# Moving two PSUM-to-SBUF copies of the softmax normalization from ScalarE to VectorE in an attention and FFN kernel

## The chip, the cores and the metric

The kernel runs on 8 NeuronCores of one Trainium2 chip. Each core takes one sequence of the batch of 8, with no exchange between cores. The metric is the device time in microseconds of the slowest core. A core has TensorE (matmuls; PE in the profile), ScalarE (ACT), VectorE (DVE), GpSimd (POOL) and SyncE (SP), which run their own instruction streams and wait for each other by semaphores; here GpSimd and SyncE only issue DMAs.

## What is computed

One transformer layer on x of shape (8, 4096, 1024), with 16 heads of 64. The reference, cut to what matters:

```python
q = _split_heads(x @ Wq + bq, h)
k = _split_heads(x @ Wk + bk, h)
v = _split_heads(x @ Wv + bv, h)
pattern = jnp.einsum('bhid,bhjd->bhij', k, q) * scale
prob = jax.nn.softmax(pattern, axis=-2)
out = jnp.einsum('bhis,bhid->bhsd', prob, v)
attn = concat @ Wo + bo
x = _layernorm(x + attn)
h = jax.nn.gelu(jnp.einsum('bse,eh->bsh', x, w1) + b1, approximate=False)
x = _layernorm(x + jnp.einsum('bsh,he->bse', h, w2) + b2)
```

## The kernel before

The kernel is written engine by engine: `tr.op("pe", ...)` appends an instruction to one engine's list and `tr.wait("pe", sem, value)` a wait in front of what comes next in that list. The order in which the Python code calls them is therefore the order of each engine's queue. On ScalarE and VectorE every instruction also waits for the one before it on the same engine (`AUTO_CHAIN`).

**First part (0 to about 750 us).** x is transposed, q, k and v are computed and written to scratch in HBM, and the weights are cast to bf16. The change does not touch it.

**Second part.** The 4096 queries are cut in 8 chunks (`qc`) of 512, and the 16 heads are taken in 8 pairs (`p`). So there are 64 head-pair blocks. In a block the keys come in 32 chunks (`kc`) of 128. For each of them TensorE computes the scores of both heads (`scores`, L799) into one of two PSUM tiles `ps_s`; ScalarE takes the exponential of a 128x1024 tile (`do_exp`, L812) into one of two SBUF tiles `es_sb`; TensorE then adds into `ps_o` the product with v (`pv`, L822) and into `ps_d` the product with ones, which is the softmax's denominator (`denom`, L834). In the loop over `kc` the order on TensorE is pv(kc), denom(kc), scores(kc+2).

`ps_o` and `ps_d` are single PSUM tiles. At the end of a block (L860 to L877) they are copied to SBUF (`dD_sb` at L864, `oO_sb` at L865), VectorE takes the reciprocal of `dD_sb` (L867) and multiplies it with `oO_sb` for the two heads (L869, L872) into `o_sb`. The value `norm_done` stands for the second copy; `pv(0)` of the next block waits for it (L819), since it writes `ps_o` again. Ahead of `pv(0)` stand, on TensorE, scores(0) and scores(1) of the next block. On ScalarE exp(0) of the next block stands behind the two copies.

**The work pumped in between.** While the blocks of chunk `qc` run, a generator (`make_post`) emits the rest of the layer for chunk `qc-1`: output projection (L635), layer norm (`emit_ln_tail`, L553 to L609), first FFN matmul (L668, eviction on VectorE at L679), Gelu on ScalarE in two batches of 128x8192 (L686), second FFN matmul (L712, L724), second layer norm (L606) and four output transposes (L741) with their copies (L747) and the DMA of the single buffer `out_sb`. `pump(n)` takes n pieces from it: one after every odd `kc` (kc = 31 too), two more at kc = 3, and one at the very end of a block, after the normalization. That makes 19 pieces per block; the generator has 107, so the pieces end within the block p = 5, and chunk `qc` = 0 has none. At the boundary behind block p (its last pumped piece before the normalization and the one after it) stand: for p = 0 two pieces of the first layer norm's last loop, for p = 1 two chunks of the first FFN matmul, for p = 2 the last such chunk with the second Gelu and a piece of the second matmul, for p = 3 two pieces of the second matmul, for p = 4 an empty piece and the start of the second layer norm's last loop, for p = 5 and 6 nothing. Behind p = 7 the 8 loads of the next chunk's `q_sb` are issued on GpSimd when the last block's matmuls are done.

Of the kernel before, what the change touches and what calls it, by code (L numbers as in the profile page):

```python
# [75 lines left out]
def build(debug=(), phases="AB", nqc=NQC, nst=NST, sparts="LTAV"):  # L76
# [36 lines left out]
    with ExitStack() as st0:  # L113
        tr = Tracer(nc, st0)
        SB = lambda *a: st0.enter_context(nc.sbuf_tensor(*a))
        PS = lambda *a: st0.enter_context(nc.psum_tensor(*a))
        pe, act, dve = "PE", "ACT", "DVE"
# [356 lines left out]
        dD_sb = SB("dD_sb", [128, 512], F32)  # L474
        oO_sb = SB("oO_sb", [128, 512], F32)

        ps_s = [PS("ps_s0", [128, 1024], F32), PS("ps_s1", [128, 1024], F32)]
        ps_o = PS("ps_o", [128, 512], F32)
        ps_d = PS("ps_d", [128, 512], F32)
# [29 lines left out]
        norm_done = 0  # L509
        o_last = 0  # L510
# [6 lines left out]
        def load_kv(p):  # L517
            b = p % 2
            tr.wait("gp", pe, free_k[b])
            v_k[b] = tr.op("gp", lambda e, p=p, b=b: e.dma_start(  # L520
                k_sb[b][:], bass.AP(k_d.tensor, p * 128 * S, [[S, 128], [1, S]])),
                sem=f"s_k{b}", n=16)
            tr.wait("gp", pe, free_v[b])
            v_v[b] = tr.op("gp", lambda e, p=p, b=b: e.dma_start(
                v_sb[b][:], bass.AP(v_d.tensor, p * 128 * S, [[S, 128], [1, S]])),
                sem=f"s_v{b}", n=16)
# [230 lines left out]
        def pump(n=1):  # L757
            nonlocal post_gen
            for _ in range(n):
                if post_gen is None:  # L760
                    return
                try:
                    next(post_gen)
                except StopIteration:
                    post_gen = None
                    return

        def load_q(qc):
            nonlocal v_q
            tr.wait("gp", pe, free_q)  # L770
            for pc in range(NP):
                v_q = tr.op("gp", lambda e, pc=pc, qc=qc: e.dma_start(
                    q_sb[:, pc * 512:(pc + 1) * 512],
                    bass.AP(q_d.tensor, pc * 128 * S + qc * 512, [[S, 128], [1, 512]])),
                    sem="s_qb", n=16)

        for qc in qc_range:
            post_gen = make_post(qc - 1) if qc > 0 else None
            if qc == 0:
                tr.wait("pe", dve, v_ones64)  # L780
                load_q(0)
                load_kv(0)
                load_kv(1)
            for p in range(NP):
                b = p % 2
                if 1 <= p < NP - 1:
                    load_kv(p + 1)
                elif p == NP - 1 and qc + 1 in qc_range:
                    load_kv(0)
                sc_done = {}  # L790
                exp_done = {}

                def scores(kc, p=p, b=b):
                    if kc == 0:
                        tr.wait("pe", f"s_k{b}", v_k[b])
                        tr.wait("pe", "s_qb", v_q)
                    v = None
                    for hh in range(2):
                        fn = lambda e, p=p, b=b, kc=kc, hh=hh: e.matmul(  # L799
                            ps_s[kc % 2][:, hh * 512:(hh + 1) * 512],  # L800
                            k_sb[b][hh * 64:(hh + 1) * 64, kc * 128:(kc + 1) * 128],
                            q_sb[hh * 64:(hh + 1) * 64, p * 512:(p + 1) * 512],
                            start=True, stop=True, tile_position=(hh * 64, 0))
                        v = tr.op("pe", fn, sem=(pe if hh == 1 else None))
                    sc_done[kc] = v

                def do_exp(kc):
                    esb = kc % 2
                    tr.wait("act", pe, es_free.get(esb, 0))
                    tr.wait("act", pe, sc_done[kc])  # L810
                    exp_done[kc] = tr.op(
                        "act", lambda e, kc=kc, esb=esb: e.activation(  # L812
                            es_sb[esb][:], ps_s[kc % 2][:], AF.Exp, scale=SCALE))

                def pv(kc, p=p, b=b):
                    tr.wait("pe", act, exp_done[kc])
                    if kc == 0:
                        tr.wait("pe", f"s_v{b}", v_v[b])
                        tr.wait("pe", act, norm_done)  # L819
                    esb = kc % 2  # L820
                    for hh in range(2):
                        tr.op("pe", lambda e, b=b, kc=kc, esb=esb, hh=hh: e.matmul(  # L822
                            ps_o[hh * 64:(hh + 1) * 64, :],
                            v_sb[b][:, kc * 128 + hh * 64: kc * 128 + (hh + 1) * 64],
                            es_sb[esb][:, hh * 512:(hh + 1) * 512],
                            start=(kc == 0), stop=(kc == NKC - 1),
                            skip_group_check=True,
                            tile_position=(0, hh * 64)))

                def denom(kc):  # L830
                    esb = kc % 2
                    v = None
                    for hh in range(2):
                        fn = lambda e, kc=kc, esb=esb, hh=hh: e.matmul(  # L834
                            ps_d[hh * 64:(hh + 1) * 64, :],
                            ones64[:],
                            es_sb[esb][:, hh * 512:(hh + 1) * 512],
                            start=(kc == 0), stop=(kc == NKC - 1),
                            skip_group_check=True,
                            tile_position=(0, hh * 64))  # L840
                        v = tr.op("pe", fn, sem=(pe if hh == 1 else None))
                    return v

                scores(0)
                do_exp(0)
                scores(1)
                vmm = 0
                for kc in range(NKC):
                    pv(kc)
                    vmm = denom(kc)  # L850
                    es_free[kc % 2] = vmm
                    if kc + 2 < NKC:
                        scores(kc + 2)
                    if kc + 1 < NKC:
                        do_exp(kc + 1)
                    if kc % 2 == 1:
                        pump(1)
                    if kc == 3:
                        pump(2)
                free_k[b] = vmm  # L860
                free_v[b] = vmm
                tr.wait("act", pe, vmm)
                tr.wait("act", dve, o_last)
                tr.op("act", lambda e: e.copy(dD_sb[:], ps_d[:]))  # L864
                norm_done = tr.op("act", lambda e: e.copy(oO_sb[:], ps_o[:]))  # L865
                tr.wait("dve", act, norm_done)
                tr.op("dve", lambda e: e.reciprocal(r_sb[:], dD_sb[:]))  # L867
                pcol = p * 512
                tr.op("dve", lambda e, pcol=pcol, qc=qc: e.tensor_tensor(  # L869
                    o_sb[qc % 2][0:64, pcol:pcol + 512],  # L870
                    oO_sb[0:64, :], r_sb[0:64, :], ALU.mult))
                o_last = tr.op("dve", lambda e, pcol=pcol, qc=qc: e.tensor_tensor(  # L872
                    o_sb[qc % 2][64:128, pcol:pcol + 512],
                    oO_sb[64:128, :], r_sb[64:128, :], ALU.mult))
                if p == NP - 1:
                    free_q = vmm
                pump(1)  # L877
            o_ready[qc] = o_last
            if qc + 1 in qc_range:
                load_kv(1)  # L880
                load_q(qc + 1)
            while post_gen is not None:
                pump(4)
# [56 lines left out]
```

How the kernel before makes its waits and increments, by code:

```python
    def wait(self, stream, sem, value):  # L49
        if value <= 0 or sem not in self.semh:
            return
        h = self.semh[sem]
        self.streams[stream].append(lambda e, h=h, v=value: e.wait_ge(h, v))
# [3 lines left out]
    def op(self, stream, fn, sem=None, n=1):  # L57
        ch = self.AUTO_CHAIN.get(stream)
        if ch is not None:
            self.wait(stream, ch, self.semv[ch])
            if sem is None:
                sem, n = ch, 1
            assert sem == ch
        if sem is None:
            self.streams[stream].append(fn)
            return None
        if sem not in self.semh:
            self._mk(sem)
        self.semv[sem] += n
        h = self.semh[sem]
        self.streams[stream].append(
            lambda e, fn=fn, h=h, n=n: fn(e).then_inc(h, n))
        return self.semv[sem]
```

## Time and profile before

| what | value |
|---|---|
| two timed runs | 4686.57 and 4742.26 us, median 4714.41 |
| the profiled execution | 4687.85 us |
| its span on the slowest core (core 4) | 4686.1 us |
| spans of the 8 cores | 4664.0 to 4686.1 us |
| TensorE busy | 3631.7 us (78%), 19264 matmuls |
| ScalarE busy | 2382.2 us (51%), 2319 instructions |
| VectorE busy | 1403.3 us (30%), 1814 instructions |
| mean granted TensorE clock, core 4 | 0.899 of 2.4 GHz |

The span runs from the first to the last instruction of a core; the time of an execution holds it and about 2 us around it. Matmul ends are modelled, so two matmuls in a row may overlap in the rows. A row's "idle before" is the time that its engine did nothing ahead of it, and behind "<-" stands what ended that idle time. A granted clock of 1.00 is 2.4 GHz, and where the engine is throttled it runs at 1.2 GHz; a value between is a mean over a stretch with both.

### The profile page before, as it was taken

The numbers are of one execution on the slowest core, as the hardware profiler recorded it, in microseconds if no ns is written. First come the engines' busy times: TensorE is split into PE (matmuls) and PEld (weight loads), VectorE is DVE, ScalarE is ACT, GpSimd is POOL, SyncE is SP. The second block draws the span as 40 slices with busy tenths as digits, with TensorE's granted clock in tenths as the row PEclk, the third lists the DMA queues.
The fourth block names the chain that finished last, engine by engine and source line by source line (L and its number), as shares of the span: only waits on it lengthen the run. The fifth ranks groups of instructions, "written<-read, shape, count | busy, mean of one in ns | idle before, by whom it ended". The sixth has DMA issues, their size and how long they took to land.

```text
span 4686.1 us, 57913 instructions; the slowest of 8 cores (4664.0 to 4686.1 us)
## 1 busy us (share of the span) xinstructions
PE 3631.7 (78%) x19264; PEld 1205.7 (26%) x19264; DVE 1403.3 (30%) x1814; ACT 2382.2 (51%) x2319; POOL 194.3 (4%) x344
## 2 busy tenths in 40 slices
PE   5365697777897799778887888788878887888766
PEld 2132242222232233222222222222222222222222
DVE  1132341114222422332233323332323232423243
ACT  0000005885557555755576556665666556655610
POOL 0010100000000000000000000000000000000000
PEclk9677798998999899989998999899999998989987
DMA  8766422113432243123412342234222322332143
GB/s 175 177 156 161 122 65 93 55 55 90 108 77 77 84 102 90 71 89 82 110 59 84 91 110 68 84 86 104 79 84 79 90 82 90 89 84 84 50 91 76
DMA packets 746248, 433.77 MB, mean 93 GB/s; under 512 B 679269, under 2 KB 695781, under 8 KB 728553
## 3 DMA queue, kind: packets, MB, share of 16 engines
q1 hardware_dynamic: 706714, 237.12, 20.6%
q0 software_dynamic: 39248, 192.96, 13.9%
q8 instruction: 164, 2.69, 0.3%
q14 instruction: 122, 1.00, 0.1%
HBM read 377.59 MB, written 77.59 MB: 97 GB/s over the span
## 4 chain that ended last, share of the span: by engine, by line
PE 61%; ACT 16%; DMA 9%; DVE 6%; issue 6%; POOL 1%; ACTq 0%; SPq 0%; DVEq 0%; POOLq 0%
ACT es_sb L812 12%; PE ps_o L822 12%; PE ps_s L799 10%; PE ps_d L834 7%; PE ps_w L712 5%; PE ps_w L668 5%; PE ps_g L712 5%; PE ps_g L668 5%; PE psq L318 3%; PE psq L422 2%; ACT h_sb L686 2%; PE psv L345 2%; DMA xt_f<-xtf_b 2%; DMA wcast<-w 2%; DMA y<-out_sb 1%
## 5 line engine op out<-in xcount | busy, mean ns | idle before, releaser
L812 ACT ACTIVATE es_sb<-ps_s 128x1024 bf16<-128x1024 f32 x2048 | 2097.4, 1024 | 1381.5 <-PE ps_s L799 1232.5
L822 PE MATMUL ps_o<-es_sb,v_sb 128*64 128x512 bf16 x4096 | 874.3, 417 | 399.9 <-ACT es_sb L812 399.4
L799 PE MATMUL ps_s<-q_sb,k_sb 64*128 64x512 bf16 x4096 | 832.3, 409 | 106.1 <-DMA q_sb<-q_scr 86.1
L834 PE MATMUL ps_d<-es_sb,ones 128*64 128x512 bf16 x4096 | 853.6, 400 | 0.0
L822 PEld LDWEIGHTS ps_o<-es_sb,v_sb 128*64 128x64 bf16 x4096 | 257.5, 108 | 1057.0 <-issue 1054.1
L867 DVE RECIPROCAL r_sb<-dD_sb 128x512 f32<-128x512 f32 x64 | 214.6, 3353 | 1037.8 <-ACT oO_sb L865 1037.1
L799 PEld LDWEIGHTS ps_s<-q_sb,k_sb 64*128 64x128 bf16 x4096 | 193.6, 94 | 997.9 <-issue 997.9
L712 PE MATMUL ps_w<-h_sb,w_sb 128*128 128x512 bf16 x1024 | 260.9, 406 | 77.2 <-ACT h_sb L686 77.2
L668 PE MATMUL ps_w<-h1b_sb,w_sb 128*128 128x512 bf16 x1024 | 259.5, 399 | 44.3 <-DVE h1b_sb L602 36.9
L278 ACT COPY xtf_b<-pst 128x512 f32<-128x512 f32 x64 | 37.5, 587 | 478.2 <-PE pst L270 277.6
L834 PEld LDWEIGHTS ps_d<-es_sb,ones 128*64 128x64 bf16 x4096 | 260.5, 112 | 2.9
L668 PE MATMUL ps_g<-h1b_sb,w_sb 128*128 128x512 bf16 x1024 | 243.7, 381 | 1.2 <-DMA w_sb<-w_scr 1.0
L712 PE MATMUL ps_g<-h_sb,w_sb 128*128 128x512 bf16 x1024 | 238.6, 380 | 0.0
L679 DVE TENSOR_SCALAR hpre_sb<-ps_w,b_pp 128x512 bf16<-128x512 f32 x128 | 96.1, 751 | 388.6 <-PE ps_w L668 316.4
L270 PE MATMUL pst<-id_f,xnat 128*128 128x128 f32 x256 | 53.4, 370 | 202.5 <-ACT xtf_b L278 173.0
L679 DVE TENSOR_SCALAR hpre_sb<-ps_g,b_pp 128x512 bf16<-128x512 f32 x128 | 96.1, 751 | 294.4 <-PE ps_g L668 286.4
L520 POOL DMA_DIRECT2D k_sb<-k_scr x64 | 34.0, 532 | 3269.3 <-PE ps_d L834 1854.8
L318 PE MATMUL psq<-xt_bf,wq_sb 128*128 128x512 bf16 x512 | 128.9, 419 | 33.6 <-DVE xpart L289 33.6
L712 PEld LDWEIGHTS ps_w<-h_sb,w_sb 128*128 128x128 bf16 x1024 | 96.9, 102 | 216.3 <-issue 129.8
L668 PEld LDWEIGHTS ps_w<-h1b_sb,w_sb 128*128 128x128 bf16 x1024 | 94.5, 101 | 179.4 <-issue 93.2
L686 ACT ACTIVATE h_sb<-hpre_sb 128x8192 bf16<-128x8192 bf16 x16 | 112.5, 7029 | 30.0 <-DVE hpre_sb L679 29.8
L668 PEld LDWEIGHTS ps_g<-h1b_sb,w_sb 128*128 128x128 bf16 x1024 | 92.2, 98 | 124.5 <-issue 29.6
(94 smaller groups left out, 2225.4 us busy)
## 6 DMA issues: line engine op xcount, KB each, us to landing
k_sb<-k_scr POOLq DMA_DIRECT2D x64, 1024.0 KB, 5.2
v_sb<-v_scr POOLq DMA_DIRECT2D x64, 1024.0 KB, 7.5
w_sb<-w_scr SPq DMA_DIRECT2D x256, 256.0 KB, 3.0
w_sb<-w_scr SPq DMA_DIRECT2D x128, 512.0 KB, 4.4
xnat<-x SPq DMA_DIRECT2D x8, 2048.0 KB, 12.3
xt_f<-xtf_b SPq DMA_DIRECT2D x64, 256.0 KB, 2.2
w_scr<-wcast SPq DMA_DIRECT2D x64, 256.0 KB, 3.7
wo_sb<-wo_scr SPq DMA_DIRECT2D x64, 256.0 KB, 3.8
```

What stands on the lines that cost most here:

```text
L318: fn = lambda e, fc=fc, cc=cc, stp=stp, qb=qb: e.matmul(psq[qb][:], wq_sb[:, cc * E + fc * 128: cc * E + (fc + 1) * 128], xt_bf[cc][:, stp ...
L345: tr.op("pe", lambda e, j=j, cc=cc, stp=stp, vb=vb, half=half: e.matmul(psv[vb][:, half * 512:(half + 1) * 512], xt_bf[cc][:, stp * 512 + ...
L422: fn = lambda e, fc=fc, cc=cc, stp=stp, qb=qb: e.matmul(psq[qb][:], wk_sb[:, cc * E + fc * 128: cc * E + (fc + 1) * 128], xt_bf[cc][:, stp ...
L668: fn = lambda e, cc=cc, wb=wb, pb=pb: e.matmul(pwb[pb][:], w1_sb[wb][:, cc * 128:(cc + 1) * 128], h1b_sb[:, cc * 512:(cc + 1) * 512], star ...
L679: last_pw[pb] = tr.op("dve", lambda e, hc=hc, pb=pb: e.tensor_scalar(hpre_sb[:, (hc % 16) * 512:(hc % 16 + 1) * 512], pwb[pb][:], b1_pp[:, ...
L686: "act", lambda e, hc=hc: e.activation(h2_sb[:, (hc - 15) * 512:(hc + 1) * 512], hpre_sb[:], AF.Gelu))
L712: fn = lambda e, hc=hc, wb=wb, pb=pb: e.matmul(pwb[pb][:], w2_sb[wb][:, (hc % 16) * 128:(hc % 16 + 1) * 128], h2_sb[:, hc * 512:(hc + 1) * ...
L799: fn = lambda e, p=p, b=b, kc=kc, hh=hh: e.matmul(ps_s[kc % 2][:, hh * 512:(hh + 1) * 512], k_sb[b][hh * 64:(hh + 1) * 64, kc * 128:(kc + ...
L812: "act", lambda e, kc=kc, esb=esb: e.activation(es_sb[esb][:], ps_s[kc % 2][:], AF.Exp, scale=SCALE))
L822: tr.op("pe", lambda e, b=b, kc=kc, esb=esb, hh=hh: e.matmul(ps_o[hh * 64:(hh + 1) * 64, :], v_sb[b][:, kc * 128 + hh * 64: kc * 128 + (hh ...
L834: fn = lambda e, kc=kc, esb=esb, hh=hh: e.matmul(ps_d[hh * 64:(hh + 1) * 64, :], ones64[:], es_sb[esb][:, hh * 512:(hh + 1) * 512], start= ...
L867: tr.op("dve", lambda e: e.reciprocal(r_sb[:], dD_sb[:]))
```

## The change

The two copies at the end of a block move from ScalarE's list to VectorE's, directly ahead of the reciprocal. With them the waits change: VectorE waits for the last `denom` itself, no longer for ScalarE's copy, ScalarE waits for nothing at this place, and `pv(0)` waits for VectorE's counter instead of ScalarE's.

```diff
@@ -816,7 +816,7 @@
                     tr.wait("pe", act, exp_done[kc])
                     if kc == 0:
                         tr.wait("pe", f"s_v{b}", v_v[b])
-                        tr.wait("pe", act, norm_done)
+                        tr.wait("pe", dve, norm_done)
@@ -859,11 +859,9 @@
                 free_k[b] = vmm
                 free_v[b] = vmm
-                tr.wait("act", pe, vmm)
-                tr.wait("act", dve, o_last)
-                tr.op("act", lambda e: e.copy(dD_sb[:], ps_d[:]))
-                norm_done = tr.op("act", lambda e: e.copy(oO_sb[:], ps_o[:]))
-                tr.wait("dve", act, norm_done)
+                tr.wait("dve", pe, vmm)
+                tr.op("dve", lambda e: e.tensor_copy(dD_sb[:], ps_d[:]))
+                norm_done = tr.op("dve", lambda e: e.tensor_copy(oO_sb[:], ps_o[:]))
                 tr.op("dve", lambda e: e.reciprocal(r_sb[:], dD_sb[:]))
```

On ScalarE, from the end of the first part on, the blocks of chunk 0 stand like this before (`es_sb` is the exponential, one block is x32):

```order
L278 COPY xtf_b<-pst 128x512 x64
L812 ACTIVATE es_sb<-ps_s 128x1024 x32
L864 COPY dD_sb<-ps_d 128x512
L865 COPY oO_sb<-ps_o 128x512
L812 ACTIVATE es_sb<-ps_s 128x1024 x32
L864 COPY dD_sb<-ps_d 128x512
L865 COPY oO_sb<-ps_o 128x512
```

and after the change, up to the first Gelu of chunk 1:

```order
L278 COPY xtf_b<-pst 128x512 x64
L812 ACTIVATE es_sb<-ps_s 128x1024 x275
L575 ACTIVATE stB<-stA 1x512
L577 ACTIVATE stA<-stB 1x512
L812 ACTIVATE es_sb<-ps_s 128x1024 x50
L686 ACTIVATE h_sb<-hpre_sb 128x8192
```

The exponentials of one block now follow directly on those of the block before. Line numbers ahead of L862 are the same in both kernels; behind it they are 2 lower after the change (the copies are L863 and L864, the reciprocal L865).

On VectorE the boundary behind block p = 1 of chunk 1 stands like this before, between evictions of the first FFN matmul (`hpre_sb`):

```order
L679 TENSOR_SCALAR hpre_sb<-ps_w,b_pp 128x512
L867 RECIPROCAL r_sb<-dD_sb 128x512
L869 TENSOR_TENSOR o_sb<-oO_sb,r_sb 64x512
L872 TENSOR_TENSOR o_sb<-oO_sb,r_sb 64x512
L679 TENSOR_SCALAR hpre_sb<-ps_g,b_pp 128x512
```

and after the change:

```order
L679 TENSOR_SCALAR hpre_sb<-ps_w,b_pp 128x512
L863 COPY dD_sb<-ps_d 128x512
L864 COPY oO_sb<-ps_o 128x512
L865 RECIPROCAL r_sb<-dD_sb 128x512
L867 TENSOR_TENSOR o_sb<-oO_sb,r_sb 64x512
L870 TENSOR_TENSOR o_sb<-oO_sb,r_sb 64x512
L679 TENSOR_SCALAR hpre_sb<-ps_g,b_pp 128x512
```

The copies stand behind the eviction of the piece pumped at kc = 31 and ahead of that of the piece pumped after the normalization.

## Rows read from the trace of the kernel before

**Rows 1.** The page's chain that ended last, shares by engine.

```profile
PE 61%; ACT 16%; DMA 9%; DVE 6%; issue 6%; POOL 1%; ACTq 0%; SPq 0%; DVEq 0%; POOLq 0%
```

**Rows 2.** Groups of instructions by line: busy us, mean ns | idle before, releasers.

```profile
L864 ACT COPY dD_sb<-ps_d 128x512 f32<-128x512 f32 x64 | 37.5, 586 | 71.5 <-PE ps_d L834 60.1 <-DVE hpre_sb L679 9.6 <-PE ps_s L799 1.3
...
L357 DVE CAST v_b<-psv 128x1024 bf16<-128x1024 f32 x32 | 39.2, 1224 | 102.1 <-PE psv L350 95.7 <-DMA v_scr<-v_b 6.3
...
L591 DVE COPY mrb_sb<-ps_g 128x512 f32<-128x512 f32 x16 | 11.1, 692 | 1.6
```

**Rows 3.** Chain of waits, 949 to 953 us (bare boundary): start us, us, what.

```profile
949.42 0.59 ACT dD_sb L864
...
950.09 0.59 ACT oO_sb L865
...
950.77 1.03 ACT es_sb L812
```

**Rows 4.** Timeline of the same boundary, TensorE: start us, us, instruction, [idle before].

```profile
948.81 0.41 PE L834 MATMUL ps_d<-es_sb,ones 128*64 128x512 bf16 x2
...
949.15 0.61 PE L799 MATMUL ps_s<-q_sb,k_sb 64*128 64x512 bf16 x4
...
952.15 0.41 PE L822 MATMUL ps_o<-es_sb,v_sb 128*64 128x512 bf16 x2 [2.39 <-ACT es_sb L812]
```

**Rows 5.** The 21 stretches between bare boundaries: us, busy us, PEclk, DMA, GB/s.

```profile
788.12:828.86 40.74, 32.44 (x194) 8.52 (x196) 4.73 (x3) 33.94 (x34) 1.05 (x2) 0.92 0.14 52
...
949.22:988.22 39.00, 30.09 (x194) 8.44 (x196) 4.72 (x3) 33.94 (x34) 1.05 (x2) 1.00 0.14 55
...
sum 841.65, PE 665.82 PEld 178.11 DVE 99.25 ACT 712.77 POOL 22.14; mean PE 31.71 PEld 8.48 DVE 4.73 ACT 33.94 POOL 1.05
```

**Rows 6.** The 14 us behind boundary p = 1, first of 14.

```profile
1201.58:1215.60 14.02, 12.70 (x67) 4.71 (x68) 7.72 (x7) 6.57 (x8) 1.05 (x2) 1.00 0.76 229
```

**Rows 7.** Timeline of VectorE, then TensorE, boundary p = 1 of chunk 2.

```profile
1682.74 0.75 DVE L679 TENSOR_SCALAR hpre_sb<-ps_w,b_pp 128x512 bf16<-128x512 f32 x1 [2.07 <-PE ps_w L668]
1683.60 3.35 DVE L867 RECIPROCAL r_sb<-dD_sb 128x512 f32<-128x512 f32 x1
...
1688.64 0.75 DVE L679 TENSOR_SCALAR hpre_sb<-ps_g,b_pp 128x512 bf16<-128x512 f32 x1
...
1686.08 0.41 PE L822 MATMUL ps_o<-es_sb,v_sb 128*64 128x512 bf16 x2 [1.32 <-ACT es_sb L812]
...
1691.45 1.90 PE L668 MATMUL ps_g<-h1b_sb,w_sb 128*128 128x512 bf16 x8
```

**Rows 8.** Timeline of VectorE, then TensorE, after boundary p = 0 of chunk 2.

```profile
1624.61 3.35 DVE L867 RECIPROCAL r_sb<-dD_sb 128x512 f32<-128x512 f32 x1 [3.11 <-ACT oO_sb L865]
...
1637.60 0.43 DVE L602 CAST h1b_sb<-h1f_sb 128x512 bf16<-128x512 f32 x1
...
1638.39 1.89 PE L668 MATMUL ps_w<-h1b_sb,w_sb 128*128 128x512 bf16 x8 [2.65 <-DVE h1b_sb L602]
```

**Rows 9.** Timeline of VectorE, then TensorE, after boundary p = 4 of chunk 2.

```profile
1896.34 0.69 DVE L591 COPY mrb_sb<-ps_g 128x512 f32<-128x512 f32 x1
1898.16 3.35 DVE L867 RECIPROCAL r_sb<-dD_sb 128x512 f32<-128x512 f32 x1 [1.13 <-ACT oO_sb L865]
...
1915.13 0.69 DVE L606 TENSOR_TENSOR h1f_sb<-sq_sb,mrb_sb 128x512 f32<-128x512 f32 x1
...
1916.39 0.66 PE L741 MATMUL ps_w<-id_f,h1f_sb 128*128 128x128 f32 x4
...
1921.55 0.63 PE L741 MATMUL ps_w<-id_f,h1f_sb 128*128 128x128 f32 x4 [2.31 <-DMA y<-out_sb]
```

**Rows 10.** Timeline: ScalarE behind p = 2, TensorE behind p = 7.

```profile
1769.33 1.28 ACT L812 ACT_TABLE_LOAD   x1 [3.26 <-PE ps_s L799]
...
1081.10 1.04 PE L799 MATMUL ps_s<-q_sb,k_sb 64*128 64x512 bf16 x4 [14.24 <-DMA q_sb<-q_scr]
```

**Rows 11.** A stretch of the first FFN matmul after its wait for `h1b_sb`.

```profile
1157.70:1169.20 11.50, 11.44 (x56) 3.55 (x58) 2.17 (x3) 4.10 (x4) 0.00 (x0) 0.85 0.20 46
```

## The prediction

> **What bounds the kernel now.** I began with the page's chain of work that ended last: TensorE holds 61% of it and ScalarE 16%, VectorE 6% [rows 1]. That is an average over unlike stretches, so I looked at the one place where the moved copies stand, the boundary between two head pairs, after `denom(31)` of one pair and before `pv(0)` of the next. There are 64, and they are of several kinds. The chain of waits through a boundary in which nothing of the FFN is pumped reads copy of `ps_d`, copy of `ps_o`, exp(0), then `ps_o` matmul, without a hole [rows 3]: ScalarE works through two copies of 0.59 us before it may start the exp that TensorE needs. TensorE has its scores done in 0.61 us and then sits idle for 2.39 us [rows 4]. So at such a boundary ScalarE's queue sets the pace. Inside a pair ScalarE paces as well (one exp per about 1.1 us), so what is won at the boundary isn't taken back by the following exps.
>
> The second thing at this place is the clock of TensorE. The stretches from one such boundary to the next last 39.00 us where the granted clock is 1.00 (2.4 GHz all through) and 40.74 where it is 0.92, since the engine fell to 1.2 GHz for a part of it [rows 5]. The 2.39 us at the boundary are the only long idle in such a stretch. There are 21 such stretches (7 in the first query chunk, p = 5 and 6 in the seven others); 18 of them show a clock under 1.00, and their sum is 841.65 us [rows 5]. At 39.00 each they would take 819.0, so the low clock costs 22.7 us there.
>
> **The change, part by part.** *Two copies leave ScalarE.* 64 times 2 copies of 586 ns [rows 2], 75 us of ScalarE. *Two copies come to VectorE.* The trace has this form, PSUM to SBUF, 128x512 f32, at line 591: 692 ns [rows 2]. Two with the 0.10 us between VectorE's instructions (1682.74 + 0.75 = 1683.49, next at 1683.60 [rows 7]) are 1.48 us. VectorE no longer waits for ScalarE before the reciprocal. *The wait of `pv(0)`* is now for VectorE's second copy, and ScalarE's copies waited for nothing else that mattered.
>
> *Bare boundary, VectorE idle (21 of them).* Take the one at 949.22, where `denom(31)` ends (948.81 + 0.41 [rows 4]). ScalarE answered 0.20 us later, at 949.42 [rows 3]. VectorE starts then too if it answers as fast, ends the copies at 950.90, and TensorE can go 0.36 us later, as after the cast that ends at 1638.03 (matmul at 1638.39 [rows 8]): 951.26. exp(0) now starts after scores(0), whose pair ends at about 949.54, plus about 0.16: 949.70 to 950.72; plus the 0.35 from the end of exp to the matmul (951.80 [rows 3] to 952.15 [rows 4]) 951.07. The later one counts: 951.26 against 952.15 [rows 4], so 0.89 us are saved and the new last wait is VectorE's copy, by 0.19 us. 21 x 0.89 = 18.7 us. Bounds of the copy: were it as short as ScalarE's, exp(0) would decide and 1.08 us be saved; were it as long as VectorE's 128x1024 cast out of PSUM, 1224 ns [rows 2], `pv(0)` would start at 952.32, 0.17 later than now. I take 0.69, since the row has the same shape, type and memories.
>
> *Boundary p = 0 of chunks 1 to 7 (7).* TensorE also gains 0.89 us here, but it runs into the layer norm: at the first `ps_w` matmul of line 668 it sits idle 2.65 us for the last cast of `h1b_sb`, which ends at 1638.03 at the end of an unbroken row of VectorE work from the reciprocal at 1624.61 on [rows 8]. The reciprocal started 1.63 us after `denom(31)` (ScalarE's second copy ends at 950.68, 1.46 us after it [rows 3], and VectorE follows in 0.17); now it starts at 0.20 + 1.48 + 0.10 = 1.78. The gain is swallowed, and the row ends 0.15 us later: 7 x 0.15 = 1.1 us lost.
>
> *Boundary p = 4 (7).* VectorE is still at line 591 until 1897.03, so the copies run to 1898.61 and the reciprocal starts at 1898.71 instead of 1898.16, 0.55 later. The second layer norm ends at 1915.82 [rows 9]; now at 1916.37, and the first transpose of line 741, at 1916.39 before, comes at 1916.73. Behind it TensorE waits for the output DMA of the single `out_sb` (idle 2.31 us before the next transpose [rows 9]), so this delay is handed on and the gain at the boundary lost: 7 x 0.35 = 2.5 us lost.
>
> *Boundaries p = 1 and 3 (14).* 16 matmuls of the FFN stand between `denom(31)` and the scores, TensorE idles only 1.32 us and for exp(0) [rows 7]. At p = 1 VectorE first has an eviction that ends at 1683.49; the copies end at 1685.07, TensorE could start at 1685.43, before 1686.08. Nothing gained or lost. The eviction behind the normalization slips from 1688.64 to about 1690.2 and ends at 1690.97; the matmul that needs its bank starts at 1691.45 [rows 7]. That cover is thin, 0.48 less 0.36 us; if it goes, some tenths of a us are lost seven times.
>
> *Boundaries p = 2 (7) and p = 7 (7).* At p = 2 exp(0) waits for scores behind the Gelu and a table load, which starts at 1769.33, 3 us after the copies ended [rows 10]; at p = 7 TensorE idles 14.24 us for `q_sb` [rows 10]. Both hide the copies before and after. Nothing. The last boundary adds 0.15 us before the final output projection.
>
> Direct sum: 18.7 - 1.1 - 2.5 - 0.1 = 15.0 us.
>
> *The clock.* The idle at the bare boundary shrinks from 2.39 to 1.50 us. Where it is 1.32 us today (p = 1 and 3) the granted clock stays at 1.00 in the 14 us from the boundary on, in all 14 places (the first is shown [rows 6]), though TensorE is denser around those (busy 12.7 of 14 us). 1.50 is much nearer to the 1.32 that never drops it than to the 2.39 that did 18 times in 21. I take three quarters of the 22.7 us back: 17 us; the bounds are 0 and 22.7.
>
> The page TensorE: Matmul & The Clock Gate of the Trainium skill (section A second HAM failure mode: psum-queue depth-cycling) says that short, frequent idles of TensorE between groups of matmuls make its clock swing between the levels. By it a boundary with 1.5 us idle could still drop it, the second case below; the rows of p = 1 and 3 disagree with it, the 18 of 21 agree.
>
> Against the profiled execution: 4687.85 (span 4686.1) - 15.0 - 17 = 4656 us, 0.7% less. The two timed runs of before are 4686.57 and 4742.26, median 4714.41: the profiled one lies at the low end, and the same saving from the median would give 4682. Differences within 2% (94 us) are about what a measurement of this kernel can't tell from no change.
>
> **The rivals.** *B, the clock still falls.* The copies leave the path, but the idle of 1.50 us drops the clock as before. For it: 18 of 21 today, with loosely packed matmuls. Against it: rows 6. 4687.85 - 15.0 = 4673.
>
> *C, slower: the stretches of layer norm and FFN give it back.* Place: p = 0 and p = 4. TensorE reaches line 668 up to 0.89 us earlier plus what the clock gave, and waits 3.5 us or more instead of 2.65 for VectorE. What follows are dense matmuls, where a drop costs more; one such stretch after the wait had a clock of 0.85 over 11.5 us [rows 11], that is 3.4 us at 1.2 GHz and 1.7 us lost. One more such drop at each of 14 places costs 24 us; if at the same time nothing comes back at the bare boundaries, -15 + 24 = +9: 4697. It decides from 9 extra drops on (15 / 1.7). Against it: six of the seven FFN stretches already begin at 0.85, so most have paid. The long copy of 1224 ns would end at the same side: 21 x 0.17, and 1.2 us at each of 7 + 7, together +20: 4708.
>
> *D, all of it.* exp(0) decides, no drop is left, and VectorE's slip hides: 21 x 1.08 + 22.7 = 45.4: 4642. The change does what it says in any case: ScalarE's row of exps is unbroken in the new order.
>
> **How the numbers follow.** Forecast 0.52, B 0.20, D 0.13, C together with the long copy 0.12, anything else 0.03. Range 4636 to 4710: D less 6 us, since the cores of one execution lie 22 us apart, up to the long copy, which also covers B and C from an execution nearer to the median. Faster by over 2% would need 94 us, twice D: 0.03. Slower by over 2% would need 1.5 us at every one of the 64 boundaries: 0.02. Within 2%: 0.95.
>
> **What would show it.** At bare boundaries: `ps_o` idle near 1.5 us, released by VectorE's `oO_sb`; copies of 0.69 us starting 0.20 us after `denom(31)`; stretches of 38.1 us at clock 1.00. At p = 0: idle before line 668 up to 3.5 us, reciprocal 1.78 us after `denom(31)`. It is wrong if the copy takes over 0.8 us, if bare stretches stay above 39 us (the clock), if a new wait shows at line 668 behind p = 1, or if the sum of the 21 stretches falls by less than 15 us.

## The result, and the profile after the change

The changed kernel takes 4662.2 us (median of 27 runs) against 4692.21 us for the kernel before (26 runs). The ratio is 0.9923, with a 95% interval from 0.9903 to 0.9943: 0.8% less time, a small difference but clear of the noise. Executions in which the cores of one die ran longer at a lower clock than the other's are left out of every ratio in this document (not out of the medians), and where too few others were left no ratio is given. The profiled execution of the changed kernel took 4654.42 us.

From the page of the changed kernel, its head, the engines and the shares of the chain that ended last:

```profile
span 4652.6 us, 57786 instructions; the slowest of 8 cores (4623.5 to 4652.6 us)
...
PE 3600.3 (77%) x19264; PEld 1204.8 (26%) x19264; DVE 1491.7 (32%) x1942; ACT 2305.6 (50%) x2191; POOL 193.7 (4%) x344
...
PE 59%; ACT 14%; DVE 10%; DMA 9%; issue 6%; POOL 1%; ACTq 0%; DVEq 0%; SPq 0%; POOLq 0%
```

VectorE's share of the chain rose from 6% to 10% and ScalarE's fell from 16% to 14% [rows 1]. The groups by line (busy us, mean ns | idle before, releasers) price the moved work:

```profile
L863 DVE COPY dD_sb<-ps_d 128x512 f32<-128x512 f32 x64 | 44.3, 692 | 847.2 <-PE ps_d L834 845.1
L864 DVE COPY oO_sb<-ps_o 128x512 f32<-128x512 f32 x64 | 44.2, 691 | 6.6
```

A copy costs 692 ns on VectorE, 106 ns more than on ScalarE, exactly the row of line 591 [rows 2]. At a bare boundary the profile's chain of waits now names VectorE (start, us, what):

```profile
942.70 0.23 PE ps_d L834 x2
...
943.09 0.70 DVE dD_sb L863
943.89 0.70 DVE oO_sb L864
944.59 0.19 issue
944.77 0.41 PE ps_o L822 x2
```

And the timeline of the same place, all three engines:

```profile
942.85 0.60 PE L799 MATMUL ps_s<-q_sb,k_sb 64*128 64x512 bf16 x4
943.09 0.69 DVE L863 COPY dD_sb<-ps_d 128x512 f32<-128x512 f32 x1 [31.11 <-PE ps_d L834]
943.40 2.14 ACT L812 ACTIVATE es_sb<-ps_s 128x1024 bf16<-128x1024 f32 x2 [1.25 <-PE ps_s L799]
943.89 0.69 DVE L864 COPY oO_sb<-ps_o 128x512 f32<-128x512 f32 x1
944.77 0.41 PE L822 MATMUL ps_o<-es_sb,v_sb 128*64 128x512 bf16 x2 [1.32 <-DVE oO_sb L864]
```

TensorE's idle is 1.32 us instead of 2.39 [rows 4]. The profile puts its end down to VectorE's second copy, since that is what ended last (944.58). But the last wait is still exp(0), by 0.05 us. In front of `pv(0)` stand three waits in TensorE's list: for exp(0), for `v_sb` and, behind them, for the copy. From the end of exp(0) to the matmul it is 0.356 us before the change, where the copies had long ended, and 0.356 us after it (medians over the 8 cores): the copy adds nothing. When the copy does decide, as in e2 below, the matmul follows it by 0.146 us; here it follows by 0.198.

The windows of the 21 bare stretches (us, busy of each engine, PEclk, DMA share, GB/s), first one and sum:

```profile
792.34:829.98 37.64, 30.09 (x195) 8.43 (x196) 6.11 (x5) 32.75 (x32) 1.05 (x2) 1.00 0.15 57
...
sum 790.60, PE 631.71 PEld 176.17 DVE 128.26 ACT 687.72 POOL 22.03; mean PE 30.08 PEld 8.39 DVE 6.11 ACT 32.75 POOL 1.05
```

All 21 of this core are at a clock of 1.00 (on the eight cores together 160 of 168; before the change 41 of 168), and their sum fell from 841.65 [rows 5] to 790.60 us. Something was given back at p = 0, at the first `ps_w` matmul of line 668 (to be read against [rows 8]):

```profile
1612.23 3.35 DVE L865 RECIPROCAL r_sb<-dD_sb 128x512 f32<-128x512 f32 x1
...
1625.22 0.43 DVE L602 CAST h1b_sb<-h1f_sb 128x512 bf16<-128x512 f32 x1
...
1626.01 3.57 PE L668 MATMUL ps_w<-h1b_sb,w_sb 128*128 128x512 bf16 x8 [4.50 <-DVE h1b_sb L602]
```

The wait is 4.50 us where it was 2.65, and the eight matmuls behind it take 3.57 us where they took 1.89.

To compare whole kernels I cut each core's timeline at the end of the last `denom` of every head pair, and take the mean over the eight cores, in us. "At 1.2 GHz" is the time in which the clock records show the lower level.

| | before | after |
|---|---|---|
| span | 4673.5 | 4635.9 |
| 21 bare stretches | 836.9 | 791.4 |
| of them at 1.2 GHz | 76.8 | 3.4 |
| stretches p = 0 (7) | 408.1 | 416.7 |
| p = 1 (7) | 513.4 | 512.1 |
| p = 2, 3 (7 each) | 999.0 | 999.6 |
| p = 4 (7) | 352.4 | 355.1 |
| p = 7 (6), and p = 7 of chunk 0 | 518.2 | 516.8 |
| up to the first boundary, and from the last | 1045.2 | 1044.0 |

A stretch "p" begins at the end of head pair p. Behind p = 1, 2 and 4 the cut stands some 0.4 us too early in every kernel, at the end of `denom(30)` (1680.23 in the kernel before, where `denom(31)` ends at 1680.66). So the rows p = 0 come out 3 us too short and those of p = 4 some 3 us too long, in all kernels alike; cut at `denom(31)`, p = 0 takes 411.2 and 419.8 us and p = 4 349.0 and 352.0. The differences between kernels hold. The bare stretches gain 45.5 us, p = 0 and p = 4 lose 8.6 and 2.7, the rest moves by a few: 37.6 in all.

### The profile page after: what moved, and what is told of

It is laid out like the page before. It is cut to its first block, busy times and chain, and to the rows that moved or that the text cites. A ratio compares the mean times of both kernels' runs of the same rounds, so it can differ in the third digit from the quotient of the medians.

```text
span 4652.6 us, 57786 instructions; the slowest of 8 cores (4623.5 to 4652.6 us)
## 1 busy us (share of the span) xinstructions
PE 3600.3 (77%) x19264; PEld 1204.8 (26%) x19264; DVE 1491.7 (32%) x1942; ACT 2305.6 (50%) x2191; POOL 193.7 (4%) x344
## 4 chain that ended last, share of the span: by engine, by line
PE 59%; ACT 14%; DVE 10%; DMA 9%; issue 6%; POOL 1%; ACTq 0%; DVEq 0%; SPq 0%; POOLq 0%
ACT es_sb L812 11%; PE ps_o L822 11%; PE ps_s L799 9%; PE ps_d L834 7%; PE ps_w L668 5%; PE ps_w L712 5%; PE ps_g L712 5%; PE ps_g L668 5%; PE psq L318 3%; PE psq L422 2%; ACT h_sb L686 2%; PE psv L345 2%; DMA xt_f<-xtf_b 2%; DMA wcast<-w 2%; DVE r_sb L865 2%
## 5 line engine op out<-in xcount | busy, mean ns | idle before, releaser
L822 PE MATMUL ps_o<-es_sb,v_sb 128*64 128x512 bf16 x4096 | 858.6, 409 | 373.0 <-ACT es_sb L812 313.7
L799 PE MATMUL ps_s<-q_sb,k_sb 64*128 64x512 bf16 x4096 | 818.5, 402 | 106.4 <-DMA q_sb<-q_scr 85.4
L834 PE MATMUL ps_d<-es_sb,ones 128*64 128x512 bf16 x4096 | 837.7, 392 | 0.0
L863 DVE COPY dD_sb<-ps_d 128x512 f32<-128x512 f32 x64 | 44.3, 692 | 847.2 <-PE ps_d L834 845.1
L865 DVE RECIPROCAL r_sb<-dD_sb 128x512 f32<-128x512 f32 x64 | 214.5, 3352 | 6.9 <-DVE oO_sb L864 0.5
L724 DVE SCALAR_TENSOR_TENSOR y_sb<-ps_w,b_pp,h1f_sb 128x512 f32<-128x512 f32 x32 | 24.0, 751 | 325.6 <-PE ps_w L712 324.9
```

Source lines behind the costliest of these rows:

```text
L799: fn = lambda e, p=p, b=b, kc=kc, hh=hh: e.matmul(ps_s[kc % 2][:, hh * 512:(hh + 1) * 512], k_sb[b][hh * 64:(hh + 1) * 64, kc * 128:(kc + ...
L822: tr.op("pe", lambda e, b=b, kc=kc, esb=esb, hh=hh: e.matmul(ps_o[hh * 64:(hh + 1) * 64, :], v_sb[b][:, kc * 128 + hh * 64: kc * 128 + (hh ...
L834: fn = lambda e, kc=kc, esb=esb, hh=hh: e.matmul(ps_d[hh * 64:(hh + 1) * 64, :], ones64[:], es_sb[esb][:, hh * 512:(hh + 1) * 512], start= ...
```

## The experiments

My theory: the gain has two terms, about 1 us of latency at each bare boundary and a clock that no longer falls there; and it is limited by VectorE's row of work at p = 0 and p = 4. The rivals: the clock is only a passenger of the order; the thin covers at p = 1 and p = 4 (little time between VectorE's work and the matmul that needs it) matter more; the loss at p = 0 is VectorE's 0.13 us and not the clock.

**e1: the kernel before, with TensorE's idle filled.** The extra matmuls' results are used nowhere.

```diff
             scores(1)
+            if (qc == 0 and p >= 1) or (qc > 0 and p >= 6):
+                tr.wait("pe", dve, last_pw[1])
+                for _ in range(6):
+                    tr.op("pe", lambda e, p=p, b=b: e.matmul(
+                        ps_g[:], k_sb[b][:, 0:128],
+                        q_sb[:, p * 512:(p + 1) * 512],
+                        start=True, stop=True))
```

> The kernel before, with six extra matmuls (bf16, 128x512, into ps_g, which nothing reads then) on TensorE between scores(1) and pv(0) at the 21 bare boundaries. They fill 1.3 us of the 2.39 us idle and shorten no wait; pv(0) still starts 2.93 us after denom(31). Theory (the clock is a term of its own): with 1.1 us idle the clock stays at 1.00 in the 21 stretches, their sum falls from 836.9 (mean of the cores before) to about 819 or less, and the time falls by some 18 us (ratio about 0.996). Rival (the gain of the change comes only from the shorter wait): the stretches keep their 837 us and the ratio is 1.000, or above it by the extra work.

Measured: ratio 0.9948 [0.9933, 0.9963]. ScalarE's copies stand where they stood, and still the bare stretches fall from 836.9 to 816.6 us (mean of the cores). Windows of one core:

```profile
909.82:948.55 38.73, 31.50 (x201) 8.94 (x202) 4.73 (x3) 33.94 (x34) 1.05 (x2) 1.00 0.14 55
948.55:987.56 39.01, 31.49 (x201) 8.93 (x202) 4.73 (x3) 33.94 (x34) 1.05 (x2) 1.00 0.14 54
...
sum 816.84, PE 661.46 PEld 187.09 DVE 99.24 ACT 712.79 POOL 22.05; mean PE 31.50 PEld 8.91 DVE 4.73 ACT 33.94 POOL 1.05
```

No stretch is below 1.00. On none of the eight cores is there any time at 1.2 GHz in them. The clock is a term of its own, of 20.3 us; the remaining 25.2 us down to the 791.4 of the change are what the moved copies bring beside the clock. (The mean span of the profiled execution is only 10.9 us shorter, 4662.6 us: its first part, which has the same code, happened to take 5.7 us more.) Two lengths, 38.73 and 39.01 us, stand at the same clock; the last section takes that up.

**e2: VectorE's copies back on the path.** The change, with the first copy made twice.

```diff
                 tr.op("dve", lambda e: e.tensor_copy(dD_sb[:], ps_d[:]))
+                tr.op("dve", lambda e: e.tensor_copy(dD_sb[:], ps_d[:]))
                 norm_done = tr.op("dve", lambda e: e.tensor_copy(oO_sb[:], ps_o[:]))
```

> The changed kernel, with the copy of ps_d made twice on VectorE ahead of the copy of ps_o. pv(0) at the bare boundaries moves from 1.86 to 2.65 us after denom(31), the idle from 1.32 to 2.11. Theory: 0.79 us lost directly at each of 21 boundaries (16.6 us), and the clock falls again at more than half of them (0.6 to 1.7 us each, some 10 to 20 us); with 0.8 us at the layer norm boundaries the ratio to before is about 1.000 to 1.003. Rival (clock untouched by the idle below the old 2.39): 16.6 + 5.5 us lost, ratio 0.997, granted clock 1.00 in all 21 stretches.

Measured: ratio 1.0042 [1.0022, 1.0061], slower than before. Windows of one core:

```profile
788.34:826.73 38.39, 30.03 (x194) 8.39 (x196) 6.80 (x6) 32.80 (x32) 1.05 (x2) 1.00 0.16 55
826.73:865.99 39.26, 31.30 (x195) 8.47 (x196) 6.80 (x6) 32.80 (x32) 1.05 (x2) 0.96 0.15 54
...
1023.25:1063.52 40.27, 32.54 (x193) 8.48 (x192) 6.80 (x6) 32.80 (x32) 1.05 (x2) 0.92 0.14 53
...
sum 824.89, PE 656.65 PEld 177.11 DVE 142.81 ACT 688.72 POOL 22.04; mean PE 31.27 PEld 8.43 DVE 6.80 ACT 32.80 POOL 1.05
```

The waits at one boundary of the same core:

```profile
945.15 2.14 ACT L812 ACTIVATE es_sb<-ps_s 128x1024 bf16<-128x1024 f32 x2 [1.25 <-PE ps_s L799]
...
946.43 0.69 DVE L865 COPY oO_sb<-ps_o 128x512 f32<-128x512 f32 x1
...
947.27 0.64 PE L822 MATMUL ps_o<-es_sb,v_sb 128*64 128x512 bf16 x2 [2.06 <-DVE oO_sb L865]
```

The stretch at full clock grows from 37.64 to 38.39 us, by 0.75, though VectorE's copies end 0.79 us later (0.69 and the 0.10 between instructions). The missing 0.05 is the margin by which exp(0), and not the copy, had been the last wait in the change; now it is the copy. TensorE's idle is 2.06 us, 0.05 less than the 2.11 expected; the low level is back (16 of the 21 stretches of this core are below 1.00; 77.5 us of it as the mean of the cores, as before), and nothing is left of the clock term. Against the change, VectorE's longer row also costs 12.5 us at p = 4, 5.7 at p = 1 and 3.3 at p = 0.

**e3b: VectorE's row longer, the path not.** One more instruction of 0.69 us behind the second copy; the reciprocal overwrites its result. (A first form, e3, wrote to a tile of its own, for which SBUF has no room: 2048 B are needed and 1824 left. It gave no time.)

```diff
                 norm_done = tr.op("dve", lambda e: e.tensor_copy(oO_sb[:], ps_o[:]))
+                tr.op("dve", lambda e: e.tensor_tensor(
+                    r_sb[:], dD_sb[:], dD_sb[:], ALU.mult))
                 tr.op("dve", lambda e: e.reciprocal(r_sb[:], dD_sb[:]))
```

> The changed kernel, with one more VectorE instruction of 0.69 us (dD_sb times itself into r_sb, overwritten by the reciprocal) behind norm_done and ahead of the reciprocal. pv(0) at the bare boundaries stays at 1.86 us. Theory (VectorE's row decides at p = 0 and 4): the first matmul of line 668 at p = 0 and the transposes at p = 4 come 0.79 us later, and p = 1 loses its thin cover; 12 to 20 us lost against the changed kernel, ratio to before 0.995 to 0.997, the 21 bare stretches unchanged at 791 us. Rival (the loss there comes from the clock alone): 0.992.

Measured: ratio 0.998 [0.9958, 1.0002]. The bare stretches take 795.0 us, 3.6 more than in the change; against the change p = 4 loses 14.1 us, p = 1 8.7 and p = 0 4.2, while the others gain some 8, for which I have no reason. In the waits of the slowest core (us in all, times, longest) that for the cast at p = 0 has grown and a new one, the second line, stands at p = 1, seven times:

```profile
PE ps_w L668 <- DVE h1b_sb L602: 58.8, 8, 19.0
...
PE ps_g L668 <- DVE hpre_sb L679: 3.1, 7, 0.8
```

3.1 us of waiting don't make 8.7; the time at 1.2 GHz in the stretches p = 1 rises too, from 47.8 to 65.7 us.

The ratio lies a little above the 0.995 to 0.997 expected. In mean spans 0.79 us more on VectorE between two pairs takes back 23.2 of the 37.6 us (4659.1 against 4635.9), nearly all of it away from the bare boundaries. There the path is the same, with an idle of 1.32 us, and still 37 of the 168 bare stretches show a lowered clock, 25 of them behind p = 5; in the change it was 8. So VectorE's row is a limit of its own, and I had priced the covers at p = 1 and p = 4 too low.

**e4: the reciprocal moved off VectorE's row.** The change, with the normalization of pairs 0 to 6 issued 21 key chunks later, inside the next pair.

```diff
+                    if kc == 21 and pending is not None:
+                        pending()
+                        pending = None
...
+                def normalize(pcol=p * 512, qc=qc):
+                    nonlocal o_last
...
+                if p == NP - 1:
+                    normalize()
+                else:
+                    pending = normalize
```

> The changed kernel, with the reciprocal and the two products of blocks p = 0 to 6 moved behind kc = 21 of the next block; only the two copies stay at the boundary (p = 7 as it was). Theory (the wait of 4.5 us at line 668 behind p = 0 is VectorE's reciprocal and products standing ahead of the layer norm's last four pieces): the row ends 4.7 us earlier, TensorE does not wait there, the clock stays up, 4.5 + 1.7 us saved in 7 chunks; at p = 4 the second layer norm ends 4.7 us earlier and up to 1.5 us per chunk are saved. Together 40 to 50 us, ratio to before about 0.983. Rival (something else holds line 668, or the deferred work delays the evictions it now stands among): ratio 0.99 to 1.00, with waits of TensorE for hpre_sb evictions in the profile.

Measured: ratio 0.9811 [0.9788, 0.9835], 4608.99 us: the fastest of all kernels here. Timeline and windows of p = 0 on one core:

```profile
1606.36 0.43 DVE L602 CAST h1b_sb<-h1f_sb 128x512 bf16<-128x512 f32 x1
...
1607.61 1.90 PE L668 MATMUL ps_w<-h1b_sb,w_sb 128*128 128x512 bf16 x8
```

```profile
1596.63:1649.46 52.83, 49.81 (x287) 16.11 (x288) 21.92 (x29) 32.74 (x32) 1.06 (x2) 1.00 0.35 95
...
sum 368.21, PE 348.89 PEld 112.99 DVE 153.50 ACT 229.17 POOL 7.42; mean PE 49.84 PEld 16.14 DVE 21.93 ACT 32.74 POOL 1.06
```

The cast ends 0.82 us before the matmul that reads it, no wait stands at line 668, and the clock is 1.00. p = 0 takes 368.6 us where the change alone takes 416.7 (means of the cores). The bare stretches take 2.9 us more than in the change: 31 of 168 show a lowered clock, 26 of them behind p = 5, again with an idle of 1.32 us. So the wait at line 668 was the place where the change's gain stopped.

**e5: one copy on each engine**, `ps_d` by ScalarE and `ps_o` by VectorE. `pv(0)` waits for both, which puts a fourth wait in front of it (not in the lines shown).

```diff
+                tr.wait("act", pe, vmm)
+                tr.wait("act", dve, o_last)
+                norm_a = tr.op("act", lambda e: e.copy(dD_sb[:], ps_d[:]))
                 tr.wait("dve", pe, vmm)
-                tr.op("dve", lambda e: e.tensor_copy(dD_sb[:], ps_d[:]))
                 norm_done = tr.op("dve", lambda e: e.tensor_copy(oO_sb[:], ps_o[:]))
+                tr.wait("dve", act, norm_a)
```

> The changed kernel, with the copy of ps_d back on ScalarE and the copy of ps_o on VectorE, side by side. exp(0) starts 0.88 us after denom(31) and pv(0) at 2.25 (idle 1.71 us instead of 1.32); the reciprocal starts at 0.97 instead of 1.76. Theory: 21 x 0.39 = 8 us lost directly at the bare boundaries and some more by the clock (an idle of 1.71 lies between the 1.32 that never drops it and the 2.11 that does), 5 to 12 us won at p = 0, 1 and 4 by VectorE's shorter row; ratio to before 0.990 to 0.997, granted clock under 1.00 in some of the 21 stretches, not in all. Rival (idle does not decide the clock): all 21 at 1.00.

Measured: no ratio; the profiled execution took 4666.02 us. Windows of one core:

```profile
792.54:830.65 38.11, 30.06 (x195) 8.40 (x196) 5.42 (x4) 33.36 (x33) 1.05 (x2) 1.00 0.14 56
...
947.15:986.17 39.02, 31.36 (x195) 8.47 (x196) 5.42 (x4) 33.37 (x33) 1.05 (x2) 0.96 0.15 55
...
sum 816.05, PE 650.25 PEld 176.90 DVE 113.74 ACT 700.70 POOL 22.03; mean PE 30.96 PEld 8.42 DVE 5.42 ACT 33.37 POOL 1.05
```

At a boundary of the same core:

```profile
948.03 2.14 ACT L813 ACTIVATE es_sb<-ps_s 128x1024 bf16<-128x1024 f32 x2
...
949.52 0.41 PE L824 MATMUL ps_o<-es_sb,v_sb 128*64 128x512 bf16 x2 [1.83 <-ACT es_sb L813]
```

exp(0), the first of the two (it ends at 949.06), is now behind one copy. TensorE idles 1.83 us, not the 1.71 expected: 0.46 us pass between the end of exp(0) and the matmul instead of 0.36, since the added wait stands behind that for exp(0). 13 of the 21 stretches show a lowered clock (8 stand at 1.00); on the eight cores it is 97 of 168. That is a point between the change and before, and it tells why the change is worth more than its microsecond. p = 0 takes 401.2 us, less than with either kernel.

**e7: the wait at p = 0 filled.** The change, with 16 matmuls (results unused) in front of line 668 for the layer norm that follows p = 0.

```diff
+            if pq < 7:
+                tr.wait("pe", dve, max(last_pw))
+                for _ in range(16):
+                    tr.op("pe", lambda e: e.matmul(
+                        pwb[0][:], wo_sb[0][:, 0:128], osrc[:, 0:512],
+                        start=True, stop=True))
```

> The changed kernel, with 16 extra matmuls (128x512, into ps_w, overwritten) on TensorE inside its wait of 4.5 us for h1b_sb at p = 0 of chunks 1 to 7. They end before the wait does. Theory (most of what is given back at p = 0 is the clock that this longer wait drops ahead of dense matmuls): the clock stays at 1.00 behind the wait, 6.8 us at 1.2 GHz less per chunk, that is 3.4 us x 7 = 24 us less, ratio to before about 0.987. Rival (the give-back is the later end of VectorE's row only, 0.13 us per chunk): ratio 0.992 as the changed kernel.

Measured: ratio 0.9886 [0.9857, 0.9914]; p = 0 401.9 us, 14.8 less than with the change. The cut at line 668 shows it best. Windows from its first matmul behind p = 0 to the next boundary, the second of seven and the sum, for one core each of the kernel before, of the change, and of e7:

```profile
1638.39:1680.23 41.84, 41.84 (x234) 13.96 (x236) 8.56 (x12) 22.53 (x22) 0.00 (x0) 1.00 0.31 70
...
sum 302.34, PE 302.33 PEld 99.05 DVE 60.00 ACT 157.71 POOL 0.00; mean PE 43.19 PEld 14.15 DVE 8.57 ACT 22.53 POOL 0.00
```

```profile
1626.01:1669.93 43.92, 43.92 (x234) 14.33 (x236) 8.56 (x12) 22.51 (x22) 0.00 (x0) 0.95 0.29 67
...
sum 308.10, PE 308.09 PEld 100.30 DVE 59.98 ACT 157.58 POOL 0.00; mean PE 44.01 PEld 14.33 DVE 8.57 ACT 22.51 POOL 0.00
```

```profile
1616.32:1658.16 41.84, 41.20 (x230) 13.95 (x236) 8.56 (x12) 22.53 (x22) 0.00 (x0) 1.00 0.31 70
...
sum 292.90, PE 288.45 PEld 97.69 DVE 60.00 ACT 157.73 POOL 0.00; mean PE 41.21 PEld 13.96 DVE 8.57 ACT 22.53 POOL 0.00
```

The same 234 or so matmuls take 41.84 us at clock 1.00 in two different kernels. As means over the cores, seven stretches together: from the boundary to line 668 109.0 us before, 109.4 after, 109.0 in e7; behind it 299.1, 307.3 and 292.9 us, with 14.2, 31.2 and 0.0 us at 1.2 GHz. TensorE is never idle behind the wait, so a us at half the clock costs half a us: 299.1 - 7.1 = 292.0 and 307.3 - 15.6 = 291.7. The whole difference is the clock. I had expected 24 us here, half of the 6.8 us at 1.2 GHz in each of the seven stretches, 47.8 us in all. But only 31.2 of these lie behind the wait, and half of that is all there was to win; the other 16.6 lie ahead of it. (The kernel before has more of the low level there, 29.3 us; ahead of line 668 the wait swallows it.) The mean span fell by 11.2 us only, to 4624.7: the stretches p = 1, which follow, take 518.2 us instead of 512.1, with 70.4 us at 1.2 GHz instead of 47.8. Part of the low level came back one stretch later.

**e8: ScalarE's copies kept at p = 0 only.**

```diff
+                on_act = qc > 0 and p == 0
+                if on_act:
+                    tr.wait("act", pe, vmm)
+                    tr.wait("act", dve, o_last)
+                    tr.op("act", lambda e: e.copy(dD_sb[:], ps_d[:]))
+                    norm_done = tr.op("act", lambda e: e.copy(oO_sb[:], ps_o[:]))
+                    norm_sem = act
+                    tr.wait("dve", act, norm_done)
...
```

> The changed kernel, with both copies back on ScalarE at the boundary p = 0 of chunks 1 to 7 alone. There pv(0) comes at 2.93 us again and TensorE waits about 2.6 us instead of 4.5 at line 668. Theory: the seven p = 0 stretches return from 417 us to the 408 us of before and the rest stays as changed, 6 to 9 us less, ratio to before about 0.9905. Rival (nothing at p = 0 comes from the change): 0.992 and the sum of those stretches stays at 417.

Measured: ratio 0.9912 [0.989, 0.9935], which overlaps the interval of the change; the time alone can't tell the two apart. In its profile (cores 0 to 3) the wait at line 668 is mostly back at 2.25 to 2.75 us (1.7 to 3.0 in all), p = 0 takes 404 to 409 us, and behind line 668 it is 297.9 us with 11.7 at 1.2 GHz: the loss at p = 0 is undone, as the theory has it. That the rest stays as changed didn't hold: on these cores p = 0 gives 10.4 us, but the bare stretches take 3.9 us more than in the change, p = 1 3.5 and p = 4 4.8, and their mean span is 2.5 us longer than that of the same cores in the change (4637.2 against 4634.7). Why, I can't say.

**e6: the deferral without the change**, the edit of e4 made to the kernel before.

> The kernel before (copies on ScalarE), with the reciprocal and the two products of blocks p = 0 to 6 moved behind kc = 21 of the next block, as in e4. Theory (two separate costs: ScalarE's copies at the bare boundaries, VectorE's row at p = 0): the 21 bare stretches keep their 837 us and low clock, the seven p = 0 stretches fall from 408 to about 376 us (368.6 in e4 plus 1.07 us of later pv(0) each), ratio to before about 0.992; together with the change's bare gain (45 us) that adds up to e4. Rival (the deferral is what saves everywhere): the bare stretches fall too and the ratio is near e4's 0.981.

Measured: no ratio; three executions lie at 4665.19 to 4677.17 us, beside 4683.77 and 4685.82 for the kernel before. Windows of one core, the sum of the bare stretches and that of p = 0:

```profile
sum 839.52, PE 662.72 PEld 178.02 DVE 99.24 ACT 712.79 POOL 22.04; mean PE 31.56 PEld 8.48 DVE 4.73 ACT 33.94 POOL 1.05
```

```profile
sum 383.04, PE 359.04 PEld 113.52 DVE 143.78 ACT 237.62 POOL 7.42; mean PE 51.29 PEld 16.22 DVE 20.54 ACT 33.95 POOL 1.06
```

The bare boundaries don't care for it; p = 0 does. In mean spans the change alone brings 37.6 us (4673.5 to 4635.9), the deferral alone 22.5 (4651.0), both together 84.3 (4589.2), 24 more than their sum. At p = 0 alone: the change +8.6, the deferral -25.6, both -39.5, so 22.5 of those 24 are there. Each removes what limits the other. (I had expected 376 us for p = 0 and it is 382.5: the low level that the boundary's idle of 2.39 us brings is still there, clock 0.97.)

## Why the prediction was right

Forecast 4656 us from a profiled 4687.85, a ratio of 0.9932; measured 0.9923. In mean spans 37.6 us against 32. The two main terms, latency and clock, were the right ones; the last wait at the bare boundary was named wrongly, and one loss was priced too low. Step by step:

- **The new last wait.** Wrong in what it is, near in size. I let TensorE answer VectorE's copy in 0.36 us, the time behind a cast, another place with other waits; e2 shows 0.15. VectorE starts 0.17 us after `denom(31)` instead of 0.20. So the copy would allow `pv(0)` at 1.80 us after `denom(31)` and exp(0) at 1.86, and exp(0) decides by 0.05 us, as rival D had it. `pv(0)` comes at 1.86 us, not 2.04; 2.93 before. So 1.07 us are saved per bare boundary instead of 0.89 (D: 1.08), 22.5 instead of 18.7.
- **The clock at bare boundaries.** Right for this kernel: the time at 1.2 GHz there fell from 76.8 to 3.4 us. e1 gives the whole term as 20.3 us (mean of the cores), I took 17 of 22.7. Rival B is refuted: 160 of 168 stretches stand at 1.00. But the idle that I reasoned with was 1.50 us and the real one 1.32, so what 1.50 does was never tested. And the analogy of rows 6 is looser than it looked: behind p = 1 and 3 an idle of 1.32 us lowered the clock in none of 112 places (before and after alike), at bare boundaries in 8 of 168, and in e3b and e4 in 37 and 31. The page TensorE: Matmul & The Clock Gate of the Trainium skill (section A second HAM failure mode: psum-queue depth-cycling), by which short, frequent idles make the clock swing, agrees with the idles of 1.83 (e5), 2.06 (e2) and 2.39 us here; with 1.32 us the clock fell in few places only.
- **p = 0.** The step was mis-sized. VectorE's row ends 0.13 us later in the chunk shown, as worked out (0.15). But I priced only the row: 1.1 us, where 8.6 were lost. The other 7.5 are rival C's mechanism in part, the longer wait before dense matmuls, with the low level behind it up from 14.2 to 31.2 us. C's price was right in kind (about 1.2 us a place, not 1.7), its count of places too high: seven of its 14, since p = 4 lost only 2.7 us. So it didn't turn the sign.
- **p = 4.** Forecast 2.5 us, measured 2.7 (3.0 when cut at `denom(31)`). The wait for the layer norm is new there: eight of 20.0 us in all, the longest 14.7, where that one alone stood before; the difference is 7 x 0.76. From `denom(31)` to the first transpose it is 20.27 us instead of 19.74, as the mean of all, 0.53 later where I had 0.35:

```profile
PE ps_w L741 <- DVE h1f_sb L606: 20.0, 8, 14.7
```

- **p = 1.** The thin cover held: eviction at 1679.92, matmul without a wait; exp(0) still decides [rows 7]. e2 and e3b show that 0.8 us more would have broken it.

```profile
1675.78 0.41 PE L822 MATMUL ps_o<-es_sb,v_sb 128*64 128x512 bf16 x2 [1.32 <-ACT es_sb L812]
...
1679.92 0.75 DVE L679 TENSOR_SCALAR hpre_sb<-ps_g,b_pp 128x512 bf16<-128x512 f32 x1
...
1681.14 1.90 PE L668 MATMUL ps_g<-h1b_sb,w_sb 128*128 128x512 bf16 x8
```

- **p = 2, 3, 7, tail.** Nothing of size, as forecast; with the two ends of the program the table shows 2 us less in all (and 1.3 at p = 1), which no step explains.
- **Rival D** (4642): its last wait, and its sum at the bare boundaries, 45.5 us against 45.4; but p = 0 took back 8.6.

So the total is close by luck in part. It hides offsetting errors: 3.8 us of latency, 3.3 of clock and some 3 of a term that I had not seen (the pause below), all too low, against a loss at p = 0 that I had priced 7.5 too low.

## What to carry to other kernels

When a short idle goes, look for two gains, the latency and the clock that it held down, and separate them by filling the idle with spare matmuls. When work moves to another engine, follow that engine's row to the next place where the bottleneck engine waits for it: reaching that place earlier makes the wait longer, and a longer wait before dense matmuls costs clock on top of its own length. Move what nobody waits for soon (here the reciprocal) out of that row; together with the change this brought more than twice the change alone (84.3 us against 37.6). And when the profile names what ended a wait, look at the order of the waits in the list: what ended last need not be what decided.

## What the runs showed of the hardware that I had not expected

ScalarE pauses for about 0.28 us extra in some stretches, released by nothing but itself. In the kernel before:

```profile
958.07 1.02 ACT L812 ACTIVATE es_sb<-ps_s 128x1024 bf16<-128x1024 f32 x1 [0.41 <-ACT es_sb L812]
```

That is the difference between the 38.73 and 39.01 us of e1. The slowest core of the kernel before shows 19 such pauses, that of the change 4. They go with the place in ScalarE's list: counted with its waits for semaphores, all 72 pauses that the exps in the bare stretches of e1 show (on eight cores) stand at one of two places of every 256 instructions, which are 128 apart, and those of chunk 0 follow each other by 256. A head pair had 134 such instructions and has 128 now (34 and 32 without the waits); in the bare stretches of the change no pause is seen. Their absence gave the change some 3 us that no step of mine had. What makes the pause, no run here shows.

TensorE answers a single wait in about 0.15 us (e2: copy ended at 947.12, matmul at 947.27). Each further wait that stands in its list behind the one that ends last adds about 0.1 us: exp(0) to `pv(0)` takes 0.356 us with two more waits behind it and 0.46 with three (e5).

By and large the clock fell more often behind longer idles, but the idle alone doesn't decide. Of 168 bare stretches it was lowered in none with the idle filled down to 1.00 us (e1), in 8, 37 and 31 at 1.32 us (the change, e3b, e4), in 97 at 1.83 us (e5), in 149 at 2.06 us (e2) and in 127, no longer more, at 2.39 us (before). What makes 1.32 us harmless in one place and not in another, no run here shows. In denser stretches a wait of 4.5 us lowers it too, as e7 shows.
